# Last tile taken off TensorE's stencil, z loaded on two queues, one output in each of four rounds split over ScalarE and GpSimd, and a reordered tail

## What is computed

```
x1  = x + zX*lap_x(x) + zY*lap_y(x) + zR*x*(1-x)     # reflecting borders, one zX, zY, zR per sequence
s   = tanh(x1 @ W1 + b1) @ v                         # one score per row; W1 is 512 x 128
out = x1 + (sum over allowed l of softmax_l(s) * x1[l]) / count     # per row j; type 0: l <= j
```

## Time and profile before

| | us |
|---|---|
| median of 3 runs (109.46 to 110.18) | 109.75 |
| the profiled execution, its own time | 110.17 |
| its span in the profile | 108.4 |
| busy: PE / DVE / ACT / POOL | 100.6 / 88.6 / 75.5 / 68.2 |
| DMA moved | 29.89 MB, 77.6% of 16 engines |

### The profile page before, as it was taken

How to read it: one execution, slowest core, us unless ns; L and a number is a source line. 1 busy time by engine, 2 the same in 40 slices (tenths; PEclk the granted TensorE clock), 3 DMA queues, 4 the chain that set the end, 5 groups by cost and what they waited for, 6 DMA issues and landing times. The chain is left out here.

```text
span 108.4 us, 1739 instructions
## 1 busy us (share of the span) xinstructions
PE 100.6 (93%) x416; PEld 59.6 (55%) x416; DVE 88.6 (82%) x129; ACT 75.5 (70%) x170; POOL 68.2 (63%) x86
## 2 busy tenths in 40 slices
PE   6999999989999998999899989998999999997950
PEld 3344578684675466556555655565565554664320
DVE  4489899589979999999999999999999685146680
ACT  0836576858789598769876986798789662758610
POOL 5799999989998994999599859974500100010000
PEclk9999999999999999999999999999999999999995
DMA  3899999979989999999999999984423253035574
GB/s 90 249 313 341 390 387 388 388 280 317 296 280 345 348 364 379 372 395 388 391 384 395 386 399 394 364 334 138 138 91 100 79 186 119 3 98 169 166 234 148
DMA packets 16741, 29.89 MB, mean 276 GB/s; under 512 B 1811, under 2 KB 2325, under 8 KB 16729
## 3 DMA queue, kind: packets, MB, share of 16 engines
q1 hardware_dynamic: 16668, 29.70, 77.6%
q10 hardware_dynamic: 60, 0.07, 0.2%
HBM read 21.37 MB, written 8.39 MB: 275 GB/s over the span
## 5 line engine op out<-in xcount | busy, mean ns | idle before, releaser
L1008 PE MATMUL hps<-x1T,W1s 128*128 128x512 f32 (+1 forms) x72 | 29.7, 555 | 0.3 <-ACT x1T L383 0.3
L1067 PE MATMUL U<-X,M 128*128 128x512 f32 x60 | 28.9, 602 | 0.6 <-ACT M L426 0.6
L587 POOL TENSOR_TENSOR lr<-xin 128x1020 f32<-128x1020 f32 (+1 forms) x16 | 29.3, 1832 | 0.0
L593 POOL TENSOR_TENSOR sq<-ab 128x1024 f32<-128x1024 f32 x12 | 28.3, 2362 | 1.3 <-DMA ab<-in_x 1.3
L804 DVE SCALAR_TENSOR_TENSOR outs<-U,fac,X 128x512 f32<-128x512 f32 x30 | 21.6, 747 | 9.3 <-ACT X L447 8.4
L374 ACT ACTIVATE xps<-xin,cdia,nzR 128x1024 f32<-128x1024 f32 x11 | 13.3, 1207 | 9.6 <-DVE X L748 9.6
L997 PE MATMUL tps<-ident,X 128*128 128x128 f32 x132 | 17.6, 276 | 2.0 <-DVE X L748 1.9
L997 PEld LDWEIGHTS tps<-ident,X 128*128 128x128 f32 x132 | 15.0, 142 | 7.6 <-issue 4.2
L638 POOL TENSOR_TENSOR cs<-cs,e 128x2 f32<-128x2 f32 x16 | 3.1, 192 | 25.3 <-ACT e L403 24.2
L1008 PEld LDWEIGHTS hps<-x1T,W1s 128*128 128x128 f32 x72 | 13.0, 190 | 10.8 <-issue 10.0
L383 ACT ACTIVATE x1T<-tps 128x512 f32<-128x512 f32 x33 | 17.7, 587 | 1.4 <-PE tps L997 1.3
(11 more groups left out here) (120 smaller groups left out, 86.0 us busy)
## 6 DMA issues: line engine op xcount, KB each, us to landing
ab<-in_x SPq DMA_DIRECT2D x48, 256.0 KB, 5.1
out<-outs SPq DMA_DIRECT2D x32, 252.0 KB
xin<-in_x SPq DMA_DIRECT2D x30, 256.0 KB, 6.0
xin<-in_x SPq DMA_DIRECT2D x2, 252.0 KB
W1s<-in_L_cond_W SPq DMA_DIRECT2D x1, 256.0 KB, 5.9
xin<-in_x SPq DMA_DIRECT2D x2, 66.0 KB
xin<-in_x SPq DMA_DIRECT2D x6, 2.0 KB
out<-outs SPq DMA_DIRECT2D x1, 64.0 KB
```

The lines of the kernel that those rows point to most:

```text
L587: pool.tensor_tensor(to[:, :, 1:D - 1], src[:, :, 0:D - 2], src[:, :, 2:D], ALU.add).then_inc(s_lr, 1)
L593: pool.tensor_tensor(sq[:, p % 3, :, :], near[:, m % 2, 0, :, :], near[:, m % 2, 1, :, :], ALU.add).then_inc(s_ud, 1)
L1008: last = mm(hps[:, part], W1s[:, c, :], x1T[:, k % 2, c, part], start=(c == 0), stop=(c == DC - 1))
L1067: mm(bank(j), weights, X1[:, i, :], start=True, stop=True).then_inc(s_U, 1)
```

## The change

1. **LAST off the stencil.** Pair 16 joins `ASIDE`: no `stencil(16)` on TensorE, no square on ScalarE and no tridiagonal matrix for it; instead six near DMAs, a 128x512 add on GpSimd, `factor_of_x(16)` on ScalarE, and three instructions instead of two in `evict(16)`. `near` grows from two slots to four, so a near load waits for the `above_below` four before.
2. **z on two queues.** zX stays on ACT's queue; zY and zR are issued by SP, ahead of the first load of x. The `warm` products shrink (512, 512 | 512 becomes 512, 320 | 384 columns), and the small product for the prompt types moves from round 0 to `lengths(3)`.
3. **Shared outputs.** Outputs j = 7, 11, 15, 19 (`SHARED`) aren't computed by VectorE: ScalarE scales `U` by `fac` into the slot (`scaled`), and GpSimd adds `X1` in place one round later (`added`). Their stores move behind the near loads of the next round.
4. **Tail.** The last four weight matrices are made around carries 26 and 27; carry 31, `pooled(32)` and `output(32)` are each split in two halves of 256 columns; `factor_of_x(2k+5)` and `weights(k)` change places with carries in some rounds.

```diff
-ASIDE = (3,) + tuple(range(5, 16))
+NS = 4
+SHARED = (7, 11, 15, 19)
+HALVES = (slice(0, D // 2), slice(D // 2, D))
+ASIDE = (3,) + tuple(range(5, 17))
             def load_near(p):
                 m = aside(p)
-                if m > 2:
-                    sp.wait_ge(s_ud, m - 2)
+                if m > NS:
+                    sp.wait_ge(s_ud, m - NS)
...
             def store(j):
-                sp.wait_ge(s_o, j + 1)
+                if j in SHARED:
+                    sp.wait_ge(s_op, shared(j))
+                else:
+                    sp.wait_ge(s_o, alone(LAST) + 1 if i == LAST else alone(j))
...
+            sp.dma_start(zrow[:, 1, :], zY.rearrange("(o n) -> o n", o=1)).then_inc(s_small, 16)
+            sp.dma_start(zrow[:, 2, :], zR.rearrange("(o n) -> o n", o=1)).then_inc(s_small, 16)
             load(0)
...
+                    if h == 1 and k >= 2 and j - 1 in SHARED:
+                        store(j - 1)
                     if k >= 1:
                         store(j + 2 * h)
-                        store(j + 2 * h + 1)
+                        if j + 2 * h + 1 not in SHARED:
+                            store(j + 2 * h + 1)
...
+            def scaled(j):
+                i = in_order(j)
+                act.wait_ge(s_f, j // GB + 1)
+                act.wait_ge(s_store[j % OS], 16 * (j // OS))
+                nc.scalar.activation(outs[:, j % OS, :], bank(j), ACT.Copy, scale=fac[:, i:i + 1]).then_inc(s_os, 1)
+            def carry_last():
+                at, to = carried(LAST - 1)
+                act.wait_ge(s_U, LAST)
+                act.wait_ge(s_T, to + 1)
+                for cols in HALVES:
+                    nc.scalar.activation(X1[at:at + 1, to, cols], bank(LAST - 1)[0:1, cols], ACT.Copy).then_inc(s_cy, 1)
...
+            def added(j):
+                to = outs[:, j % OS, :]
+                pool.wait_ge(s_os, shared(j))
+                pool.tensor_tensor(to, to, X1[:, in_order(j), :], ALU.add).then_inc(s_op, 1)
...
+            def output_last():
+                to = outs[:, LAST % OS, :]
+                dve.wait_ge(s_f, KG + 1)
+                dve.wait_ge(s_store[LAST % OS], 16 * (LAST // OS))
+                for h, cols in enumerate(HALVES):
+                    dve.wait_ge(s_Uy, h + 1)
+                    vec.scalar_tensor_tensor(out=to[:, cols], in0=tps[:, h, 0:D // 2], scalar=fac[:, LAST:TILES], in1=X1[:, LAST, cols],
+                                             op0=ALU.mult, op1=ALU.add).then_inc(s_o, 1)
...
             pe.wait_ge(s_one, 1)
-            warm(512, 512)
+            warm(512, 320)
...
-            warm(512)
+            warm(384)
...
-                if 2 * k + 4 == PAIRS - 1:
-                    stencil(PAIRS - 1)
```

More of the change, by code:

```diff
@@ L155, in build @@
         s_A = sem("s_A")
-        s_near = [sem(f"s_near_slot{k}") for k in range(2)]
+        s_near = [sem(f"s_near_slot{k}") for k in range(NS)]
         s_u = sem("s_u")
@@ L224, in bank @@
                 return U[:, j % 2, :]
-            return tps[:, 0, :] if j == LAST else xps[:, j % 2, :]
+            return xps[:, j % 2, :]
         def carried(j):
@@ L259, in near_loaded, with shared, alone @@
         def near_loaded(p):
-            return 16 * sum(5 if q < NB else 4 for q in ASIDE if q <= p and (aside(q) - aside(p)) % 2 == 0)
+            return 16 * sum(6 if q == PAIRS - 1 else 4 for q in ASIDE if q <= p and (aside(q) - aside(p)) % NS == 0)
+        def shared(j):
+            return sum(q <= j for q in SHARED)
+        def alone(j):
+            return j + 1 - shared(j)
         def stored(q):
@@ L415, in exp_last, with weights @@
                                      bias=bia[:, 1:2], scale=scl[:, 1:2]).then_inc(s_e, 1)
-            def weights(k):
+            def weights(k, which=range(GB)):
                 act.wait_ge(s_e, k + 1)
@@ L423, in weights @@
                     act.wait_ge(s_msk, 2)
-                for m in range(GB):
+                for m in which:
                     i = in_order(GB * k + m)
@@ L817, in ending @@
                 factors_last()
-                output(LAST)
+                output_last()
             settings()
@@ L1064, in pooled, with pooled_last @@
                 if 2 <= j < LAST - 2:
-                    pe.wait_ge(s_o, j - 1)
-                weights = Mz[:, :] if j == LAST else M4[:, k % 2, i - GB * k, :]
-                mm(bank(j), weights, X1[:, i, :], start=True, stop=True).then_inc(s_U, 1)
+                    if j - 2 in SHARED:
+                        pe.wait_ge(s_os, shared(j - 2))
+                    else:
+                        pe.wait_ge(s_o, alone(j - 2))
+                mm(bank(j), M4[:, k % 2, i - GB * k, :], X1[:, i, :], start=True, stop=True).then_inc(s_U, 1)
+            def pooled_last():
+                pe.wait_ge(s_M, TILES)
+                pe.wait_ge(s_cz, LAST - 1)
+                for h, cols in enumerate(HALVES):
+                    pe.wait_ge(s_cy, h + 1)
+                    mm(tps[:, h, 0:D // 2], Mz[:, :], X1[:, LAST, cols], start=True, stop=True).then_inc(s_Uy, 1)
             def warm(*widths):
```

102 lines of the change are left out of this document (66 added, 36 removed).

## The result

Measured together in 20 runs each, the kernel before had a median of 109.91 us (109.46 to 111.46) and the changed kernel one of 111.03 us (109.70 to 112.46, and one run of 169.71). The comparison leaves the most disturbed runs out; its ratio of after to before is 1.0053, with a 95% interval of 1.0032 to 1.0073. By that ratio the change is within 1%, as forecast, but on the other side of zero: 0.6 us more instead of 0.1 less. The median of all runs is 1.1 us more, and at 111.03 us it lies above the forecast range of 108.4 to 110.6. The forecast also had no word on the spread. Seven of the 20 runs lie at 109.70 to 110.62, thirteen above 110.9; before, one of 20 lies above 110.2.

What follows compares the result with a forecast made beforehand. Bound: the eviction, factor, eviction loop through one PSUM tile in middle rounds, TensorE at the start, TensorE and carries late. Start -0.6, types -0.3, store 7 +0.8, rest 0 make -0.1: 109.6 us, range 108.4 to 110.6.

Steps and rivals of the forecast that it cites:

- Start: TensorE's warm-up and z's loads: fewer warm columns and two queues let the first stencil begin earlier, gain 0.6 us.
- All loads start about 0.6 us later; the first loads have more slack than that.: SP queue at the start: two tiny DMAs issued first delay all loads by 0.6 us, which the first loads can absorb.
- Middle rounds begin 0.9 us earlier.: Sum of start (0.6) and types' product (0.3) on entering the middle rounds: 0.9 us earlier, 0.5 to 1.3.
- Shared outputs (0), a gap of 1.41 us.: Second gap between evictions in a round: ScalarE's factor still sets its 1.41 us, so relieving VectorE of outputs gains 0.
- The slot of store 7: Before output 13, which reuses output 7's slot: store lands at 63.6, wait 0.8 us, leaving 0.1 us ahead whatever the start gained.
- LAST off the stencil: TensorE's path at 87.08 loses 0.86 us, but output 24, behind VectorE's later branch, holds `pooled(26)`: gain 0.
- tail: Order of the last carries, weights and outputs: about 0.3 us kept, the split halves cost 0.2 and 0.1, sum 0.
- Sum: Whole span: start -0.6, types -0.3, store 7 +0.8, the rest 0, giving -0.1 us.
- Rival (c): Hole in DMA stays unfilled, store 7 lands at 65.4 or later, output 13 waits 2.6 us: 111.4 us; chance 0.12.

Runs made afterwards that it cites:

- the repeat: The changed kernel, unaltered, run a second time for a second profile: 111.78 us.
- the first profile: The profiled execution of the changed kernel from its first measurement, with nothing altered: 112.07 us.
- the split stores: The changed kernel with every full store issued as two DMAs, of 112 and 14 rows: 111.02 us, ratio 1.0024 to the kernel before.
- the third profile: The changed kernel, unaltered, measured again beside the store-ahead and split-store kernels: median 112.16 us over six runs, the profiled one 112.05 us.

## Why the prediction was wrong, step by step

- **Start (0.6, ends 0.2 and 1.0).** This step failed, and with it the forecast of the spread. The prediction saw that "one or two stencil passes may still run slow, at 0.4 us each" and made it a discount. It is a fork: in 7 of 13 profiles the pass is fast and VectorE's first addition 0.9 to 1.1 us earlier; in 6 all four matmuls are slow, that addition comes at 8.15 (before: 8.19), and the next evictions 0.8 us and more behind before (14.90 to 15.26 against 14.08). The kernel before varies there too, without the slow pass: its start put the first addition at 8.19 in its own profile and at 7.71 in the one with the shared outputs alone. The columns taken out were counted as waste; in the long warm-up they carried TensorE past the change of pace before the first pass began. The Trainium skill ("TensorE: Matmul & The Clock Gate", Part 1, section "What's actually happening") says that the moment at which the gate opens isn't tied to the start of the kernel and so varies; the warm-up products here agree, which end their slow passes early in one execution (0.91 us for 2 x 384 columns at 4.28) and not at all in another (1.65).
- **"All loads start about 0.6 us later; the first loads have more slack than that."** Wrong for `above_below(3)`. It waited 0.15 to 1.25 us for its rows (the profile names the near loads or the load of x) in 12 of the 16 profiles with zY and zR on SyncE's queue, and in none of the three with z on ScalarE's.
- **"Middle rounds begin 0.9 us earlier."** In the changed kernel they began 0.2 earlier in the repeat and 1.45 later in the first profile. GpSimd was missing from this step: before, it idled only 0.21 us ahead of the sums of round 0 (at 23.16), so scores that come 1.6 us earlier meet an engine that can't take them. I had read VectorE and TensorE in rounds 0 and 1, not the third engine that feeds both.
- **Shared outputs (0), a gap of 1.41 us.** Right: 57.78 + 1.28 to 60.47 is 1.41, 0.75 of it idle.
- **The slot of store 7 (loss 0.8, a pin).** The mechanism was right, but the term was mis-sized, and this is what turned the sign. Forecast: store landed at 63.6, the next eviction 0.1 us ahead of before. Where rounds 0 and 1 were undisturbed: output 13 at 64.11 to 64.48, the eviction 0.4 to 0.8 us behind before (64.78, 64.79, 64.84, 65.15). The last near load landed at 63.2 to 63.6, about as computed; the sum took the store to land with it, but it came 0.9 us later. Its own 126 rows of 2 KB at 385 GB/s are an estimated 0.67 us of that. Against an execution of before with an earlier start the loss is larger: in the profile with the shared outputs alone, which has before's start, the last instruction of `evict(11)` began at 61.01, where 61.61 stood. The rule of the Trainium skill that the prediction weighed ("DMA: Bandwidth & Descriptors", section "Why a DMA increments its semaphore by 16 and not by 1") gave 64.4, nearer than the sum, though the split stores neither confirm nor refute it.
- **LAST off the stencil (0), tail (0).** Right: the branch at 94.3, output 24's first wait at 97.1, 2.8 us as before; TensorE idle for it; 25.12 us against 25.23. Leaving the branch out showed that it is what holds output 24. Not foreseen: in two of the profiles the clock fell right behind that idle time.
- **Sum.** -0.1 became +0.4 or more at the pin and -0.1 in the tail where neither the first pass nor the clock was slow; these two come on top. The pin and the tail alone would bring 109.91 to an estimated 110.2 to 110.6, still inside the range; how much of the rest of the 1.1 us each of the two costs in the median isn't measured. Rival (c), slower by an unfilled hole in DMA, didn't occur in the changed kernel, but did with the shared outputs alone (114.71), where the near slots had not been added.

Open: why long runs remained with the long warm-up in the changed kernel; how its shortest runs (109.70 to 109.88) come to equal before's median, when every profile is behind at the pin; what the single runs near 170 us are (mean clock 0.563), and the two of 114 us beside the third profile (0.958 and 0.959); where the store's last 0.2 us go; and whether the idle time in the tail is what costs the clock.

## What to carry to other kernels

When a step makes one engine's work ready earlier, read every engine that takes it up, with its idle time ahead of that very instruction. A store in a load queue is as late as the loads issued ahead of it, so put it by the time its slot is wanted. Warm-up products that end before the work begins are not spare: shorten them only as far as the slowest execution allows, and judge by many runs, since one profile shows one arm of the fork.

## What the runs showed of the hardware

- The first stencil pass took 3.78 us or 1.88 to 2.00, nothing between, in 19 profiles, while the profile's granted clock reads full speed in both cases. Only the duration tells.
- After 1.72 us of idle time TensorE's granted clock fell to 0.58 for about 4 us in one profile, and stayed at 1.00 in the repeat, where the idle time was 1.47 us. In the tail it fell after 0.97 and 1.00 us of idle time in two profiles, and stayed at 1.00 after 0.97 us in two others. So the length of the idle time alone doesn't tell.
- After this branch of VectorE 2.8 us passed until the next wait in its queue, also where it came 2.8 us later (91.5 to 94.3, and 94.3 to 97.1).
